# Attention and expert block on one core: the word lists of the five engines in another order

## The chip, the cores and the metric

The kernel runs on one core of one Trainium2 chip. The metric is the time of one execution on the device in microseconds (us), as the median of three runs. Engines are named as the profile names them: PE multiplies matrices, DVE is the vector engine, ACT the scalar engine, POOL is GpSimd, and SP issues DMAs.

## The reference

For 8 batches of 256 tokens with 128 channels the reference adds a gated attention and then a gated layer of experts. Attention has 16 heads of 8 channels and is the sum of a causal self-attention and a cross-attention to 256 context rows of 64 channels.

```python
x = x + tanh(g_xattn) * attention(layernorm(x), ctx)
x = x + tanh(g_ffn) * experts(layernorm(x))

def attention(x, ctx):
    y = softmax(causal(q @ k.T * scale)) @ v          # 16 heads, 256 x 256
    y = y + softmax(qc @ kc.T * scale) @ vc           # 16 heads, 256 x 256
    return y @ Wp + bp

def experts(x):
    s = sigmoid(x @ router.T)                         # 16 experts in 4 groups
    w = top 4 of s + bias within the best 2 groups    # each weight s, scaled to sum 2.5
    return sum over e of w[e] * (silu(x @ gate[e].T) * (x @ up[e].T)) @ down[e].T
```

## The kernel before

Each batch is one chain of small steps, and the steps of several batches overlap. Every step is a word `what:batch:n` (a number that is left out is 0), and the table ORDERS (lines 91 to 237) holds, for each engine, the list of the words that this engine executes, in exactly that order. Nothing else sets the order: there is no scheduler, the engines run their own lists and meet only at semaphores. PE has 717 words, DVE 391, ACT 378, SP 130 and POOL 110. If the first word in a list has to wait, all words behind it on that engine wait too.

The steps of one batch, with the lines of the work in the kernel before:

- *Prologue.* DVE takes the statistics of x (`stats1`, L1000, L1003), POOL makes the reciprocal deviation and the normalised x (`rstd1`, `xn1`, L586 to L593), PE transposes it (`xnT`, L852) and projects it (`proj`, L861 to L864; `vproj`, L879, L881). ACT copies the results out (`xnT_e`, `proj_e`, `v_e`). ACT, POOL and DVE split queries and keys into three bf16 parts (`part0`, L682; `sp1`, L412 and L415; `sp3`, L419). The second index 0 is cross, 1 is self.
- *Stacks.* SP and ACT store the parts to DRAM (`pd0`, `pd1`, `pd2`, L426, L427) and load them back as tall operands: `qst`, `kst` (L434, L437), and for the first batch's cross-attention in two halves of heads, `qh` and `kh`. The causal mask is stored as extra rows of the self stacks (`tri`, L485).
- *Row maxima.* For 28 chunks of scores (`max`, 0 to 15 cross L803, 16 to 27 self L800) PE makes 128x512 scores in one of two banks and DVE reduces them (`tmax`, L1011). Chunk k waits for the reduction of chunk k-2. PE then transposes the maxima (`shift`, L888), ACT copies them, and SP writes them into one row of the query stack (`shd`, L496, L498).
- *Exponentials.* For 28 chunks (`exp`, 0 to 15 cross L825, 16 to 27 self L822) PE makes the transposed scores, the row maximum already subtracted through the added row, and ACT exponentiates them (`exp_e`, L709). There are two banks, and chunk s waits for ACT's work on chunk s-2. Chunks 0 and 16 also wait for the landing of the row of maxima.
- *Values.* PE multiplies probabilities and values in four pieces (`pv`, L846), transposes the result back (`y`, L893), DVE divides by the sum (`m`, L1017, L1024), POOL adds the cross and self results (`yadd`, L607), PE transposes and projects (`yT`, `wp`, L901), DVE adds the residual (`x1`, L1132), which POOL prepared (`xres`, L601).
- *Experts.* Statistics (`stats2`), `rstd2` and `xn2` on POOL, transpose on PE (`xn2T`), router scores (`logits`, L908), tanh on ACT, the choice of four experts on DVE in 16 small steps (`route`, L1035 to L1083, the last one writes r_w), transpose of the weights on PE (`combT`, L912), and for pairs of experts `ga`, `up` (L918), `swish`, `tup` (L1091, L1099), the weights on POOL (`fhc`, L626) and `down` (L943); `out` (L1149) and `st` end the batch. For the weights `cout` and `cin` store them and load them back spread over partitions.

While one batch is in its exponentials, the next is in its row maxima and the one before in its experts. PE reads a bank called misc for transposes and projections: its uses are numbered in the order of PE's list, one after another.

```python
for what, b, n in order("pe"):        # each engine has such a loop
ge(pe, max_taken, b * NC1 + k - 1)    # a row-maximum chunk: two banks
ge(pe, exp_done, b * NC2 + s - 1)     # an exponential chunk: two banks
pe.wait_ge(comb_done, b + 1)          # combT: r_w of the batch is there
```

## Time and profile before

| | |
|---|---|
| runs of the kernel before | 346.58, 353.40, 349.49 us |
| median | 349.49 us |
| span of the profiled execution | 347.6 us |
| median less that span | 1.9 us |
| PE, DVE, ACT, POOL busy | 92%, 74%, 56%, 43% of the span |

The profiled execution's time is known as its span; what lies around the span in an execution is taken as the difference from the median. A row of a timeline has its start, its length, the engine and line, the operation with its output and inputs, how many were joined, and in brackets the time that the engine stood idle before it, with what ended that. L lines are those of the kernel before; in the changed one the table is two lines shorter, so every later line has a number lower by two.

### The profile page before, as it was taken

How to read it: one execution, taken by the hardware profiler on the slowest of the kernel's cores; microseconds unless marked ns; L12 is line 12 of the kernel's file. 1: busy time of each engine (PE TensorE's matmuls, PEld its weight loads, DVE VectorE, ACT ScalarE, POOL GpSimd, SP SyncE). 2: the span in 40 equal slices, each digit the busy share in tenths (PEclk: the TensorE clock that was granted, in tenths of full speed). 3: DMA queues.
4: the chain of work that ended last, by engine and by line, in shares of the span. 5: the costliest groups of instructions: out<-in, count | busy, mean ns of one | idle time of the engine just before them, and what ended most of it. 6: DMA issues, size and time to landing. Idle time of an engine off the chain costs nothing.

```text
span 347.6 us, 8679 instructions
## 1 busy us (share of the span) xinstructions
PE 318.1 (92%) x3186; PEld 247.7 (71%) x3186; DVE 256.4 (74%) x639; ACT 196.2 (56%) x399; POOL 151.1 (43%) x176
## 2 busy tenths in 40 slices
PE   1579599989999999999999999999999999978696
PEld 0455365666687788778887888787888787856665
DVE  4238666868898888988798888888889854748742
ACT  2433356767667765687637765675666467532041
POOL 3884061404470588047633494318410722903422
PEclk9856759999999999999999999999999999989999
DMA  4269674688563855537655365077156005214000
GB/s 123 68 183 188 146 194 115 145 209 187 199 151 103 184 131 149 143 96 151 147 139 133 88 172 140 20 152 183 34 124 141 0 18 90 37 50 88 16 1 15
DMA packets 32889, 40.45 MB, mean 116 GB/s; under 512 B 3440, under 2 KB 29824, under 8 KB 30368
## 3 DMA queue, kind: packets, MB, share of 16 engines
q1 hardware_dynamic: 32004, 38.46, 46.7%
q10 hardware_dynamic: 844, 1.45, 1.7%
q8 instruction: 25, 0.41, 0.5%
q14 instruction: 16, 0.13, 0.2%
HBM read 29.84 MB, written 7.45 MB: 107 GB/s over the span
## 4 chain that ended last, share of the span: by engine, by line
PE 76%; DVE 7%; DMA 6%; SPq 5%; POOL 2%; issue 2%; ACT 1%; POOLq 0%; DVEq 0%
PE bank L918 15%; PE bank L846 14%; PE bank L825 8%; PE bank L943 7%; PE bank L800 7%; PE bank L803 6%; PE bank L822 5%; DMA k_stack<-tri_k 4%; SPq L427 2%; PE bank L893 2%; DVE row_max L1011 2%; PE bank L861 2%; PE bank L852 2%; SPq L426 1%; PE bank L956 1%
## 5 line engine op out<-in xcount | busy, mean ns | idle before, releaser
L1011 DVE TENSOR_REDUCE row_max<-bank 128x2 f32<-128x512 f32 (+1 forms) x224 | 146.9, 686 | 43.0 <-PE bank L803 24.9
L709 ACT ACTIVATE probs<-bank 128x512 f32<-128x512 f32 x224 | 127.5, 595 | 57.5 <-PE bank L825 27.7
L918 PE MATMUL bank<-xn2T,w_pairs_sb 128*128 128x256 f32 x256 | 68.0, 392 | 1.5 <-issue 0.9
L846 PE MATMUL bank<-probs,v_ext 128*32 128x256 f32 (+1 forms) x1024 | 57.2, 365 | 0.0
L626 POOL TENSOR_TENSOR f_h<-f_h,comb 128x512 f32<-128x512 f32 x32 | 40.3, 1273 | 36.1 <-DMA comb<-c_scr 20.4
L803 PE MATMUL bank<-k_stack,q_stack 72*128 72x256 bf16 x256 | 49.9, 284 | 2.7 <-DVE row_max L1011 2.1
L918 PEld LDWEIGHTS bank<-xn2T,w_pairs_sb 128*128 128x128 f32 x256 | 44.7, 193 | 8.3 <-issue 2.8
L825 PE MATMUL bank<-q_stack,k_stack 73*128 73x256 bf16 x256 | 49.2, 284 | 1.0 <-DMA q_stack<-shiftT 0.9
L412 POOL TENSOR_TENSOR rest<-proj,part 128x512 f32<-128x512 f32 x14 | 16.2, 1160 | 74.7 <-ACT part L682 74.6
L846 PEld LDWEIGHTS bank<-probs,v_ext 128*32 128x32 f32 x1024 | 30.0, 112 | 19.9 <-issue 4.7
L800 PE MATMUL bank<-k_stack,q_stack 121*128 121x128 bf16 (+1 forms) x384 | 39.1, 231 | 2.4 <-DMA k_stack<-tri_k 1.9
L943 PE MATMUL bank<-w_down,f_h 128*128 128x128 f32 x256 | 35.9, 277 | 0.0
L822 PE MATMUL bank<-q_stack,k_stack 121*128 121x128 bf16 (+1 forms) x384 | 35.4, 219 | 0.1
L800 PEld LDWEIGHTS bank<-k_stack,q_stack 121*128 121x128 bf16 (+1 forms) x384 | 29.0, 103 | 8.9 <-issue 2.8
L803 PEld LDWEIGHTS bank<-k_stack,q_stack 72*128 72x128 bf16 x256 | 22.0, 100 | 16.7 <-DVE row_max L1011 8.6
L943 PEld LDWEIGHTS bank<-w_down,f_h 128*128 128x128 f32 x256 | 31.8, 191 | 0.4
L724 ACT ACTIVATE f_tanh<-bank 128x512 f32<-128x512 f32 x32 | 19.2, 599 | 22.6 <-PE bank L918 22.6
L1091 DVE SCALAR_TENSOR_TENSOR f_gate<-f_tanh,bank 128x512 f32<-128x512 f32 x32 | 21.7, 679 | 13.7 <-ACT f_tanh L724 13.7
L822 PEld LDWEIGHTS bank<-q_stack,k_stack 121*128 121x128 bf16 (+1 forms) x384 | 27.0, 98 | 5.7 <-issue 1.7
L825 PEld LDWEIGHTS bank<-q_stack,k_stack 73*128 73x128 bf16 x256 | 23.9, 102 | 6.8 <-ACT probs L709 1.4
L607 POOL TENSOR_TENSOR y<-y,y_self 128x256 f32<-128x256 f32 x8 | 5.8, 728 | 50.1 <-DVE y_self L1024 50.1
L1099 DVE TENSOR_TENSOR f_h<-f_gate,bank 128x512 f32<-128x512 f32 x32 | 21.9, 683 | 6.0 <-PE bank L918 5.1
(113 smaller groups left out, 367.9 us busy)
## 6 DMA issues: line engine op xcount, KB each, us to landing
k_stack<-k_scr SPq DMA_DIRECT2D x45, 192.0 KB
q_stack<-q_scr SPq DMA_DIRECT2D x14, 576.0 KB
comb<-c_scr SPq DMA_DIRECT2D x14, 512.0 KB, 6.7
q_scr<-part SPq DMA_DIRECT2D x46, 64.0 KB
k_scr<-part SPq DMA_DIRECT2D x46, 64.0 KB
x_in<-in_x SPq DMA_DIRECT2D x8, 128.0 KB, 2.4
w_pairs_sb<-in_w_pairs SPq DMA_DIRECT2D x1, 1024.0 KB, 7.8
out<-y_out SPq DMA_DIRECT2D x8, 128.0 KB, 1.9
```

The lines of the kernel that those rows point to most:

```text
L626: nc.gpsimd.tensor_tensor(at, at, comb[:, 2 * j:2 * j + 2, :], ALU.mult).then_inc(f_hc_done, 1)
L709: nc.scalar.activation(probs[:, seq % NP, :], exp_bank[s % 2][:, :], ACT.Exp).then_inc(exp_done, 1)
L800: last = pe.matmul(ps[:, n, kt * 128:(kt + 1) * 128], q[0:rows_used], key[0:rows_used, kt * 128:(kt + 1) * 128], start=n == 0 and kt == 0, ...
L803: last = pe.matmul(ps[:, n, :], q[0:STACK], key[0:STACK], start=n == 0, stop=n == nh - 1)
L822: last = pe.matmul(ps[:, n, qt * 128 - q0:(qt + 1) * 128 - q0], key[0:rows_used], q[0:rows_used, qt * 128:(qt + 1) * 128], start=n == 0 an ...
L825: last = pe.matmul(ps[:, n, :], key[0:STACK + 1], q[0:STACK + 1], start=n == 0, stop=n == nh - 1)
L846: last = pe.matmul(pv_bank[32 * n:32 * n + VW, col + q0:col + T], v[:, VW // 2 * odd:VW // 2 * odd + VW], weights, start=odd == 0 and kt = ...
L918: last = pe.matmul(bank_of[:, n * T:(n + 1) * T], w[:, e0:e0 + 128], xn2T[:, :], start=True, stop=True)
L943: last = pe.matmul(gate_bank[:, n * 128:(n + 1) * 128], f_h[:, j, n * 128:(n + 1) * 128], w_down[:, j, :], start=j == 0 and n == 0, stop=j ...
L1011: nc.vector.tensor_reduce(row_max[:, kind, qt, h0:h0 + nh], max_bank[k % 2][:, :].rearrange("p (h k) -> p h k", h=nh), AX.X, ALU.max).then ...
L1091: nc.vector.scalar_tensor_tensor(out=f_gate[:, :], in0=f_tanh[:, :], scalar=1.0, in1=gate_bank[:, :], op0=ALU.add, op1=ALU.mult).then_inc( ...
L1099: nc.vector.tensor_tensor(f_h[:, 2 * j:2 * j + 2, :], f_gate[:, :].rearrange("p (n x) -> p n x", n=2), up_bank[:, :].rearrange("p (n x) -> ...
```

## The change

The five lists of ORDERS hold the same words in another order. No instruction is added, removed or altered; 523 of PE's 717 words, 229 of ACT's 378, 172 of DVE's 391, 80 of POOL's 110 and 78 of SP's 130 stand at another place, most of them by a few places. Only a handful go more than ten places: `combT:0` on PE, the statistics of batches 5 and 6 on DVE, `marks:7` and `xres:5` on POOL. Core lines of the diff (PE at the start and near the end, DVE, POOL and SP):

```diff
     'pe': '''
...
-        max:0:6 xnT:2 max:0:7 max:0:8 proj:2:1 max:0:9 max:0:10 shift:0 max:0:11 proj:2 max:0:12 max:0:13 max:0:14
-        max:0:15 shift:0:2 max:0:16 max:0:17 exp:0 max:0:18 exp:0:1 max:0:19 max:0:20 exp:0:2 max:0:21 exp:0:3 exp:0:4
+        proj:1:1 max:0:8 max:0:9 max:0:10 xnT:2 max:0:11 max:0:12 max:0:13 shift:0 max:0:14 max:0:15 proj:2:1 proj:2
+        shift:0:2 max:0:16 exp:0 exp:0:1 max:0:17 max:0:18 max:0:19 exp:0:2 exp:0:3 max:0:20 max:0:21 max:0:22 exp:0:4
...
-        pv:7:1 exp:7:18 exp:7:19 up:5:2 exp:7:20 ga:5:3 exp:7:21 up:5:3 xn2T:6 exp:7:22 exp:7:23 logits:6 pv:7:2
-        combT:6 pv:7:3 ga:6 up:6 y:7:1 ga:6:1 yT:7 up:6:1 wp:7 ga:6:2 up:6:2 ga:6:3 up:6:3 xn2T:7 logits:7 down:6
+        exp:7:18 pv:7:1 up:5:2 exp:7:19 exp:7:20 ga:5:3 exp:7:21 xn2T:6 up:5:3 exp:7:22 exp:7:23 pv:7:2 logits:6
+        pv:7:3 combT:6 ga:6 up:6 y:7:1 ga:6:1 yT:7 up:6:1 wp:7 ga:6:2 up:6:2 up:6:3 ga:6:3 xn2T:7 logits:7 down:6
...
     'pool': '''
...
-        yadd:4 fhc:3 sp1:7:1 fhc:3:1 rstd2:4 xn2:4 fhc:3:2 fhc:3:3 sp3:7:1 yadd:5 xres:6 fhc:4 fhc:4:1 rstd2:5 fhc:4:2
+        fhc:3 marks:7 rstd2:4 xres:5 fhc:3:1 fhc:3:2 xres:6 xn2:4 fhc:3:3 yadd:5 fhc:4 fhc:4:1 fhc:4:2 xres:7 rstd2:5
...
     'sp': '''
-        load:0 w:0 load:1 load:2 ones:0 pd1:0 pd2:0 load:3 kh:0 pd1:0:1 pd2:0:1 kh:0:1 pd0:1 kst:0:1 tri:0 shd:0 pd2:1
-        pd1:1 pd1:1:1 pd0:1:1 pd2:1:1 shd:0:2 qst:1 kst:1 qst:1:1 shd:0:1 pd2:2 kst:1:1 tri:0:1 pd1:2 pd0:2 pd1:2:1
+        load:0 w:0 load:1 load:2 ones:0 pd1:0 pd2:0 load:3 kh:0 kh:0:1 pd2:0:1 pd1:0:1 tri:0 kst:0:1 shd:0 pd2:1 pd1:1
+        pd0:1 pd0:1:1 pd2:1:1 pd1:1:1 qst:1 shd:0:2 kst:1 qst:1:1 shd:0:1 tri:0:1 kst:1:1 pd2:2 pd0:2 pd1:2 pd1:2:1
```

Place 1, the start, POOL before, between the normalised x of batch 1 and that of batch 2 (L601 is the residual, L580 and L582 clear the values' buffer of one batch, L412 to L419 split the first self-attention's operands):

```order
L593 TENSOR_SCALAR xn<-x_in,mean,rstd 128x128 x2
L412 TENSOR_TENSOR rest<-proj,part 128x512
L415 TENSOR_SCALAR part<-rest 128x512
L419 TENSOR_TENSOR part<-rest,part 128x512
L586 TENSOR_SCALAR rstd<-mean 128x2
L588 TENSOR_TENSOR rstd<-rstd,minus_half 128x2
L593 TENSOR_SCALAR xn<-x_in,mean,rstd 128x128 x2
```

POOL now, from the residual behind the normalised x of batch 1 to the normalised x of batch 2:

```order
L599 TENSOR_TENSOR x_res<-x_in,bp_row 128x256
L578 MEMSET v_ext 128x1536
L580 MEMSET v_ext 128x32x2
L578 MEMSET v_ext 128x1536
L580 MEMSET v_ext 128x32x2
L410 TENSOR_TENSOR rest<-proj,part 128x512
L413 TENSOR_SCALAR part<-rest 128x512
L417 TENSOR_TENSOR part<-rest,part 128x512
L599 TENSOR_TENSOR x_res<-x_in,bp_row 128x256
L584 TENSOR_SCALAR rstd<-mean 128x2
L586 TENSOR_TENSOR rstd<-rstd,minus_half 128x2
L591 TENSOR_SCALAR xn<-x_in,mean,rstd 128x128 x2
```

The second clearing and the residual of batch 1 now stand in front of the normalised x of batch 2; the first clearing stood ahead of the piece shown before.

Place 1 on DVE before, from the statistics of batch 2 (row_max is the row maximum of a chunk of batch 0):

```order
L1000 BN_STATS stats<-x_in 128x6 x2
L1003 BN_AGGR mean<-stats 128x2 x2
L1011 TENSOR_REDUCE row_max<-bank 128x2
L1000 BN_STATS stats<-x_in 128x6 x2
L1003 BN_AGGR mean<-stats 128x2 x2
L1011 TENSOR_REDUCE row_max<-bank 128x2 x6
L412 TENSOR_TENSOR rest<-proj,part 128x512
L415 TENSOR_SCALAR part<-rest 128x512
L1011 TENSOR_REDUCE row_max<-bank 128x2 x4
```

DVE now, from the same statistics:

```order
L998 BN_STATS stats<-x_in 128x6 x2
L1001 BN_AGGR mean<-stats 128x2 x2
L998 BN_STATS stats<-x_in 128x6 x2
L1001 BN_AGGR mean<-stats 128x2 x2
L1009 TENSOR_REDUCE row_max<-bank 128x2 x11
L410 TENSOR_TENSOR rest<-proj,part 128x512
L413 TENSOR_SCALAR part<-rest 128x512
L417 TENSOR_TENSOR part<-rest,part 128x512
L1009 TENSOR_REDUCE row_max<-bank 128x2 x5
```

The statistics of batch 3 went from behind the first row maximum to ahead of it, and the split of batch 1's operands from behind the seventh to behind the eleventh.

Place 2, the end, PE before, around the transposed expert weights of batch 6 (L912), the last piece of values of batch 7 (L846), the experts of batch 6 (L918) and the transpose of the self result of batch 7 (L893):

```order
L943 MATMUL bank<-w_down,f_h 128x128 x4
L912 MATMUL bank<-ident,r_w 16x128 x2
L846 MATMUL bank<-probs,v_ext 32x256 x4
L846 MATMUL bank<-probs,v_ext 32x128 x4
L846 MATMUL bank<-probs,v_ext 32x256 x4
L846 MATMUL bank<-probs,v_ext 32x128 x4
L918 MATMUL bank<-xn2T,w_pairs_sb 128x256 x4
L893 MATMUL bank<-ident,y_raw 128x128 x4
```

PE now, at the same place:

```order
L941 MATMUL bank<-w_down,f_h 128x128 x6
L844 MATMUL bank<-probs,v_ext 32x256 x4
L844 MATMUL bank<-probs,v_ext 32x128 x4
L844 MATMUL bank<-probs,v_ext 32x256 x4
L844 MATMUL bank<-probs,v_ext 32x128 x4
L910 MATMUL bank<-ident,r_w 16x128 x2
L916 MATMUL bank<-xn2T,w_pairs_sb 128x256 x4
L891 MATMUL bank<-ident,y_raw 128x128 x4
```

The values went from behind the expert weights to ahead of them.

Place 2 on DVE before, the end of the routing of batch 6 (r_eout to r_w) with the division of batch 7's cross result (recip, y) in it:

```order
L1073 MATCH_REPLACE r_eout<-r_etop,r_ein 128x20 x2
L1017 RECIPROCAL recip<-bank 128x32
L1024 TENSOR_TENSOR y<-bank,recip 128x256
L1075 SCALAR_TENSOR_TENSOR r_sel<-r_eout,r_score 128x2x16
L1078 TENSOR_REDUCE r_sum<-r_sel 128x2
L1080 RECIPROCAL r_sum<-r_sum 128x2
L1083 SCALAR_TENSOR_TENSOR r_w<-r_sel,gate,r_sum 128x32
L1149 TENSOR_TENSOR y_out<-bank,x 128x256
```

DVE now, at the same place:

```order
L1071 MATCH_REPLACE r_eout<-r_etop,r_ein 128x20 x2
L1073 SCALAR_TENSOR_TENSOR r_sel<-r_eout,r_score 128x2x16
L1076 TENSOR_REDUCE r_sum<-r_sel 128x2
L1078 RECIPROCAL r_sum<-r_sum 128x2
L1081 SCALAR_TENSOR_TENSOR r_w<-r_sel,gate,r_sum 128x32
L1015 RECIPROCAL recip<-bank 128x32
L1022 TENSOR_TENSOR y<-bank,recip 128x256
L1147 TENSOR_TENSOR y_out<-bank,x 128x256
```

The division went from the middle of the routing to behind it.

Place 3, the middle, POOL before, around the second layernorm of batch 4 (rstd, xn), with the expert weights of batch 3 (f_h):

```order
L626 TENSOR_TENSOR f_h<-f_h,comb 128x512
L586 TENSOR_SCALAR rstd<-mean 128x2
L588 TENSOR_TENSOR rstd<-rstd,minus_half 128x2
L593 TENSOR_SCALAR xn<-x,mean,rstd 128x128 x2
L626 TENSOR_TENSOR f_h<-f_h,comb 128x512 x2
L419 TENSOR_TENSOR part<-rest,part 128x512
```

POOL now:

```order
L624 TENSOR_TENSOR f_h<-f_h,comb 128x512
L612 MEMSET rest 16x1024
L614 AFFINE_SELECT rest<-rest 16x1024
L584 TENSOR_SCALAR rstd<-mean 128x2
L586 TENSOR_TENSOR rstd<-rstd,minus_half 128x2
L599 TENSOR_TENSOR x_res<-x_in,bp_row 128x256
L624 TENSOR_TENSOR f_h<-f_h,comb 128x512 x2
L599 TENSOR_TENSOR x_res<-x_in,bp_row 128x256
L591 TENSOR_SCALAR xn<-x,mean,rstd 128x128 x2
L624 TENSOR_TENSOR f_h<-f_h,comb 128x512
```

Between rstd and xn of batch 4 there now stand two residuals and two steps of expert weights.

## Rows read from the trace of the kernel before

**Rows 1.** The page's first part, busy time of each engine over the span

```profile
PE 318.1 (92%) x3186; PEld 247.7 (71%) x3186; DVE 256.4 (74%) x639; ACT 196.2 (56%) x399; POOL 151.1 (43%) x176
```

**Rows 2.** Three stretches: PE, PEld, DVE, ACT, POOL busy, PE clock, DMA share, GB/s

```profile
20.00:30.00 10.00, 9.28 (x34) 6.00 (x33) 5.04 (x12) 3.82 (x9) 8.29 (x10) 0.50 0.80 194
107.00:285.00 178.00, 177.96 (x1978) 145.95 (x1979) 149.29 (x378) 116.97 (x241) 81.73 (x85) 1.00 0.50 117
285.00:347.60 62.60, 53.98 (x424) 41.98 (x412) 35.74 (x103) 22.57 (x45) 22.68 (x23) 0.97 0.21 41
```

**Rows 3.** The chain that ended last: start us, us, what

```profile
26.75 13.16 DMA k_stack<-tri_k
...
107.19 1.86 PE bank L846 x32
...
284.48 1.86 PE bank L846 x32
```

**Rows 4.** DVE timeline, first row maxima: start us, us, line, operation [idle before]

```profile
23.83 0.69 DVE L1011 TENSOR_REDUCE row_max<-bank 128x2 f32<-128x512 f32 x1 [5.93 <-PE bank L803]
...
40.77 1.29 DVE L1011 TENSOR_REDUCE row_max<-bank 128x4 f32<-128x512 f32 x2 [3.06 <-PE bank L800]
```

**Rows 5.** Waits of DVE, 42 to 75 us: total us, times, longest us

```profile
DVE row_max L1011 <- PE bank L800: 4.8, 9, 1.7
DVE row_max L1011 <- PE bank L803: 4.7, 2, 3.2
```

**Rows 6.** POOL timeline, prologues of batches 1 and 2

```profile
10.83 0.72 POOL L601 TENSOR_TENSOR x_res<-x_in,bp_row 128x256 f32<-128x256 f32 x1
...
13.87 1.38 POOL L580 MEMSET v_ext<- 128x1536 f32 x1 [1.32 <-DVE part L419]
...
22.29 1.59 POOL L593 TENSOR_SCALAR xn<-x_in,mean,rstd 128x128 f32<-128x128 f32 x2 [0.18 <-POOL rstd L588]
```

**Rows 7.** SP timeline, DMA issues of the first stacks

```profile
22.10 1.23 SPq L437 DMA_DIRECT2D k_stack<-k_scr  x3
...
33.89 0.71 SPq L496 DMA_DIRECT2D q_stack<-shiftT  x1
```

**Rows 8.** ACT timeline, issue of the first self stack

```profile
24.34 0.78 ACTq L434 DMA_DIRECT2D q_stack<-q_scr  x1
```

**Rows 9.** Exponentials by form: duration ns min/median/max, first and last start

```profile
L709 ACT ACTIVATE probs<-bank x224: 569/597/655, 41.6 to 305.1; 128x512 f32<-128x512 f32 x112
```

**Rows 10.** POOL timeline, second layernorm of batch 4

```profile
242.14 1.59 POOL L593 TENSOR_SCALAR xn<-x,mean,rstd 128x128 f32<-128x128 f32 x2 [0.18 <-POOL rstd L588]
243.70 1.28 POOL L626 TENSOR_TENSOR f_h<-f_h,comb 128x512 f32<-128x512 f32 x1
```

**Rows 11.** PE timeline, transpose of that layernorm

```profile
246.01 0.38 PE L852 MATMUL bank<-ident,xn 128*128 128x128 f32 x2
```

**Rows 12.** PE timeline near the end

```profile
298.78 0.59 PE L908 MATMUL bank<-w_model_sb,xn2T 128*128 128x16 f32 x4
299.30 1.51 PE L846 MATMUL bank<-probs,v_ext 128*32 128x256 f32 x32
...
307.96 0.38 PE L912 MATMUL bank<-ident,r_w 128*16 128x128 f32 x2 [1.91 <-DVE r_w L1083]
308.27 2.13 PE L846 MATMUL bank<-probs,v_ext 128*32 128x256 f32 x32
310.33 3.01 PE L918 MATMUL bank<-xn2T,w_pairs_sb 128*128 128x256 f32 x8
313.18 0.60 PE L893 MATMUL bank<-ident,y_raw 128*128 128x128 f32 x4
```

**Rows 13.** DVE timeline, routing near the end

```profile
306.20 0.35 DVE L1017 RECIPROCAL recip<-bank 128x32 f32<-128x32 f32 x1
306.58 0.42 DVE L1024 TENSOR_TENSOR y<-bank,recip 128x256 f32<-128x256 f32 x1
...
307.57 0.25 DVE L1083 SCALAR_TENSOR_TENSOR r_w<-r_sel,gate,r_sum 128x32 f32<-128x32 f32 x1
```

254 lines of the change are left out of this document (126 added, 128 removed).

## The prediction

> **What bounds the kernel now.** I read the page's first part, then the same engines by stretches, then the chain of waits, and only then the timelines of the engines at the places that the change touches.
>
> The first part shows PE at 318.1 of 347.6 us and DVE at 256.4 [rows 1]. A share says little about an order; the stretches say more. From 107 to 285 us PE is busy for 177.96 of 178.00 us at the full clock, while DVE has 149.29 and POOL 81.73 [rows 2]. In that stretch nothing that another engine does can come too late for PE: a word that moves there moves PE's work about and removes none. The chain gives the same as a period. The first piece of values of a batch starts at 107.19 for one batch and at 284.48 for the one five batches on [rows 3], so (284.48 - 107.19) / 5 = 35.5 us a batch, all of it PE's own work. The order can be worth something only where PE is not full: before 107 us and after 285 us. Behind 285 us PE works for 53.98 of 62.60 us, so 8.6 us are open there [rows 2].
>
> In the start three things are to be seen. The load of the first stacks keeps the DMA engines at a share of 0.80 between 20 and 30 us, at a PE clock of 0.50 [rows 2]. The self maxima of batch 0 wait for the causal mask, which was issued at 26.75 and took 13.16 us to land [rows 3]; DVE is idle for 3.06 us just there [rows 4]. And up to 75 us DVE waits for scores from PE for 4.8 + 4.7 = 9.5 us, with a longest wait of 3.2 [rows 5]: the row maxima set the pace and they are sometimes not fed.
>
> At the end the chain is one batch's routing. The router scores of batch 6 come at 298.78, the weights r_w are ready at 307.57 + 0.25 = 307.82, PE has waited 1.91 us for them at 307.96, and the last values of batch 7 and the next experts stand behind that wait [rows 12, 13].
>
> **The change, part by part.** The multiset of words is the same, so nothing is added to or taken from any engine's work; the sum is about waits alone. It is made against the profiled span, 347.6 us, and the 1.9 us between that and the median are put back at the end.
>
> *The end.* Before, the last values of batch 7 stand behind the transposed weights: 307.96 weights, 308.27 values (2.13), 310.33 experts (3.01), 313.18 transpose of the result [rows 12]. Now the values come first. PE's other words ahead of them are the same, and they end 1.91 us before 307.96, at 306.05 [rows 12]; the values fit between 306.05 and 308.2, inside the old wait. What then counts is when r_w is there. Two edits pull at it. The router scores now stand behind the third piece of values, which takes 1.51 [rows 12]; an expert word that stood ahead of the transpose before the scores goes behind it, and I charge +1.2. On DVE the division of batch 7's cross result, 0.35 + 0.42 = 0.77, goes from the middle of the routing to behind it [rows 13]: -0.77. So r_w is ready at 307.82 + 1.2 - 0.77 = 308.25. The transposed weights follow at 308.4 for 0.38, then 8 expert matrices of up to 3.01, then the transpose at 311.7 at the latest, against 313.18: a gain of 1.5. If the expert matrices run at the full clock (2.13 us of values there against 1.51 for the same 32 matrices at 299.30, both in rows 12, so a factor of 0.7), the transpose is at 310.6 and the gain is 2.6. I take 2.0. Behind the transpose the division of the self result, the residual, the second layernorm, the routing and the experts of batch 7 follow one another as before, so the gain goes through to the end. Bounds: if the experts of batch 6 are late because their weights come behind the third values too, the 1.2 costs and only the 0.77 comes back, 0.43 lost, so +0.5; if the values fill the wait wholly and the scores are not later, the 1.91 + 0.77 and some clock: -3.0.
>
> *The start.* POOL now clears both batches' value buffers and prepares a second residual ahead of the normalised x of batch 2: one clearing of 1.38 and one residual of about 0.72 more, less the 1.32 us for which POOL waits before [rows 6]. The normalised x of batch 2 thus ends about 0.8 later than 22.29 + 1.59 = 23.88, at 24.7. DVE's statistics of batch 3 wait for that x (it reads the mean that they overwrite), and they now stand ahead of the first row maximum. That one was at 23.83 [rows 4], and is now at about 25.6, a loss of 1.8; behind it are queued the 16 cross maxima, and PE's score chunks wait for these. Against this, DVE's work up to the sixteenth maximum is the same as before, and only the place of the statistics and of batch 1's split in it differs; some of the wait for the first scores is made up where DVE waited for later ones. I take the last cross maximum to end 0.6 later. SP issues the second half of the first key stack straight behind the first half, without the two pairs of part stores that stood between, which I put at 3 to 4 us before 22.10, and the mask ahead of the self keys, which I put at 2.5 us before 26.75 [rows 3, 7]. The mask's landing was at 26.75 + 13.16 = 39.9; I take 38.3. The self queries pay for it: ACT issued them at 24.34 [rows 8], and now does so behind the self projection of batch 1, for which PE first does eight score chunks, so near 32; they should land beside the mask. The row of maxima of the first half, which SP issued at 33.89 [rows 7], comes from a transpose that now stands behind three more score chunks: near 37.5, landing near 40.5 to 41, and the first exponential starts then, as before. One wait (the mask) goes and the other (that row) takes its place within about half a us. Net zero. Bounds: if the mask was all that held the stretch, the 3.06 us of DVE's wait come back, -3; if the late first maximum passes through whole and SP's six part stores, which now stand ahead of the next stack's loads, add theirs, 1.8 + about 2, +4.
>
> Here the Trainium skill bears on the sum: "DMA: Bandwidth & Descriptors", in its section on issuing engines not being separate queues, says that DMAs from SP, ACT and GpSimd end on the same 16 engines and interleave, and that issuing from several saves only issue time. The share of 0.80 [rows 2] agrees. By that rule an earlier issue of one half only delays the other, and the term of the start would be zero; by the 13.16 us of the mask alone [rows 3] it would be the 2.5 us by which the issue is earlier.
>
> *The middle.* PE has 0.04 us of idle time in 178 [rows 2], so a gain of zero is the ceiling for all words there. What could be lost is a word that becomes ready too late. On PE the exponential chunks are now mostly in pairs; one costs ACT 0.597 us [rows 9], and with two banks the second pair waits if PE has less than about 1.2 us of other work between pairs. In the list I find a values piece, two row-maximum chunks or expert words between nearly all pairs. On POOL the second layernorm of batch 4 is now split: two residuals and two weight steps stand between its two parts, 2 x 0.72 + 2 x 1.28 = 4.0 us [rows 6, 10]. Before, the normalised x ended at 242.14 + 1.59 = 243.73 and PE transposed it at 246.01 [rows 10, 11], a reserve of 2.28, so 4.0 would leave 1.7 us of waiting. But in PE's list the transpose has gone back too by some 2 us, and its router scores with it; 0.3 or less remains. I count the middle at zero; bounds 0 and +5 (three such words at 1.7).
>
> *Sum.* 347.6 - 2.0 + 0 + 0 = 345.6 us of span, and with 1.9 around it 347.5 us.
>
> **The rivals.**
> *The start is repaired.* If the paired chunks, an earlier mask and earlier prologues of the following batches keep DVE fed before 75 us, the 3.06 [rows 4] and the 9.5 [rows 5] go in part: with half, 6.3, the time is 349.5 - 6.3 - 2.0 = 341.2 us, faster. For it: PE is not full there and DVE is asked all the time. Against it: the landing of the first stacks is a matter of bytes, and the first maximum is later, not earlier.
> *Pairs of exponentials make PE stand.* The place is PE's list from 107 to 285 us, the price up to 0.597 us per pair [rows 9], and it decides where less than 1.2 us of PE work stands between two pairs. There are about 33 more adjacent pairs than before; at 0.3 each they cost 9.9 us: 349.5 - 2.0 + 9.9 = 357.4 us, slower. For it: there is no reserve in 178 us, each wait is a loss in full. Against it: the list has such work between nearly all pairs.
> *The order hardly matters.* The gain at the end is eaten by the later scores, the rest is zero: 349.5 us.
>
> **How the numbers follow.** The forecast, 347.5, gets 0.49 with a range of its own from 344 to 351; the repaired start 0.21; the pairs, with late layernorms and late loads that work the same way, 0.16; no difference 0.14. About 2%, 7.0 us, is what a measurement of this kernel can tell from no change: its three runs lie 6.8 us apart. Faster than 342.5 is the most of the repaired start and a little of the forecast, 0.22; slower than 356.5 is most of the pairs and a little of the forecast's upper end, 0.17; the rest, 0.61, lies within. The range reaches from 340 to 357: below it lies the part of the repaired start in which more than two thirds of DVE's waits go, above it the part of the pairs in which each costs over 0.3.
>
> **What would show it right or wrong.** Right at the end: PE's wait ahead of the transposed weights is under 1 us with the values ahead of it, and the transpose of batch 7's self result follows the end of batch 5's last `down` by 4.5 to 5.6 us, where it is 313.18 - 306.05 = 7.1 before. Right at the start: the mask lands before 39.9, DVE's 3.06 us shrink, but the first exponential stays near 41 and the first values at 107 stay within 2 us. Right in the middle: the period of 35.5 us stands and PE has no idle time from 107 to 285. The prediction is wrong if the first values come at 103 or earlier (the start was repaired), or if PE shows waits for probabilities, layernorms or stacks of more than 3 us between 107 and 285 (the pairs, or the late layernorms).

## The result and the profile after

| | kernel before | changed kernel |
|---|---|---|
| median of 20 runs | 350.53 us | 354.11 us |
| lowest and highest | 346.58 to 354.74 | 350.45 to 358.55 |
| span of the profiled execution | 347.6 | 349.9 |

The ratio is 1.0104 with a 95% interval of 1.0078 to 1.0131: the new order is slower by about 1.0%, 3.6 us, less than the 2% of a clear verdict but outside the noise. Ratios and intervals, here and below, leave out those executions of a kernel that took over 1.5% more than its fastest. The profiled execution of the changed kernel took 351.63 us and is one of the quicker ones, so its span shows 2.3 us of the 3.6.

The first look is again at the stretches, which answer to [rows 2]. Behind the first column are busy time and count of PE, PEld, DVE, ACT and POOL, then PE clock, DMA share and GB/s:

```profile
20.00:30.00 10.00, 5.35 (x20) 2.67 (x18) 3.67 (x9) 2.13 (x5) 5.18 (x7) 0.50 0.82 178
107.00:285.00 178.00, 177.81 (x1972) 145.89 (x1971) 148.75 (x369) 116.12 (x241) 84.57 (x88) 1.00 0.53 123
```

The stretch from 107 to 285 us is as full as before, 177.81 of 178.00 us. From 20 to 30 us PE is busy for 5.35 us where it was for 9.28. Since the middle of this execution neither gives nor takes, everything that changed can be read as a shift between the two timelines. PE's timeline, at the first and the last batch of the middle, as the chain had them in [rows 3]:

```profile
111.65 1.72 PE L844 MATMUL bank<-probs,v_ext 128*32 128x256 f32 x28
```

```profile
288.00 1.72 PE L844 MATMUL bank<-probs,v_ext 128*32 128x256 f32 x28
```

The first values of batch 2 start at 111.65 where they started at 107.12 in the same view (the chain's row is 0.07 later), so the whole loss, 4.5 us, is there before the middle begins. The period is (288.00 - 111.65) / 5 = 35.3 us, where it was 35.5. Near the end the last `down` of batch 5, which has the same 672 words ahead of it on PE in both lists, ends 4.5 us later too (310.54 against 306.05). The span ends 2.3 us later, so 2.2 of the 4.5 are given back at the end.

**The start.** PE's timeline in the first 60 us, with the idle time before a row and what ended it in brackets:

```profile
24.76 0.61 PE L801 MATMUL bank<-k_stack,q_stack 72*128 72x256 bf16 x2 [4.11 <-DMA q_stack<-q_scr]
25.16 1.06 PE L859 MATMUL bank<-xnT,w_model_sb 128*128 128x256 f32 x2
26.01 1.06 PE L861 MATMUL bank<-ctx_in,w_ctx_sb 128*128 128x256 f32 x2
...
31.47 1.06 PE L859 MATMUL bank<-xnT,w_model_sb 128*128 128x256 f32 x2
...
39.21 0.61 PE L801 MATMUL bank<-k_stack,q_stack 72*128 72x256 bf16 x2 [2.61 <-DVE row_max L1009]
...
41.00 1.06 PE L859 MATMUL bank<-xnT,w_model_sb 128*128 128x256 f32 x2
...
43.56 0.89 PE L861 MATMUL bank<-ctx_in,w_ctx_sb 128*128 128x256 f32 x2
...
44.50 0.39 PE L798 MATMUL bank<-k_stack,q_stack 121*128 121x128 bf16 x4
44.73 0.60 PE L823 MATMUL bank<-q_stack,k_stack 73*128 73x256 bf16 x4
...
54.53 1.03 PE L823 MATMUL bank<-q_stack,k_stack 73*128 73x256 bf16 x4 [2.19 <-DMA q_stack<-shiftT]
```

PE stands for 4.11 us until the first stack is there. Its queries, in the chain, took 6.49 us:

```profile
18.23 6.49 DMA q_stack<-q_scr
```

Before, the projections of batch 1 filled that time; now the one for the cross-attention is in the rows at 25.16 and 26.01, behind the chunk that waits, and the one for the self-attention at 31.47 and 32.32, between the eighth chunk and the ninth. At 39.21 PE stands for 2.61 us for a row maximum. From 41.00 to 44.45 it makes the projections of batch 2, which now stand between the last cross chunk and the first self chunk (44.50). At 54.53 it stands for 2.19 us for a row of maxima. DVE's timeline, which answers to [rows 4], and POOL's show what holds the maxima:

```profile
25.72 0.49 DVE L998 BATCH_NORM_STATS2 stats<-x_in 128x6 f32<-128x128 f32 x2 [10.50 <-POOL xn L591]
...
26.41 0.66 DVE L1009 TENSOR_REDUCE row_max<-bank 128x2 f32<-128x512 f32 x1
...
33.85 2.09 DVE L1009 TENSOR_REDUCE row_max<-bank 128x2 f32<-128x512 f32 x3 [1.44 <-PE bank L801]
35.85 0.68 DVE L410 TENSOR_TENSOR rest<-proj,part 128x512 f32<-128x512 f32 x1
...
37.03 1.52 DVE L417 TENSOR_TENSOR part<-rest,part 128x512 bf16<-128x512 f32 x1
...
40.70 1.29 DVE L1009 TENSOR_REDUCE row_max<-bank 128x2 f32<-128x512 f32 x2 [0.16 <-PE bank L801]
44.93 1.36 DVE L1009 TENSOR_REDUCE row_max<-bank 128x4 f32<-128x512 f32 x2 [2.94 <-PE bank L798]
```

```profile
11.76 2.58 POOL L591 TENSOR_SCALAR xn<-x_in,mean,rstd 128x128 f32<-128x128 f32 x2 [0.18 <-POOL rstd L586]
...
24.02 1.59 POOL L591 TENSOR_SCALAR xn<-x_in,mean,rstd 128x128 f32<-128x128 f32 x2 [0.18 <-POOL rstd L586]
36.65 1.35 POOL L410 TENSOR_TENSOR rest<-proj,part 128x512 f32<-128x512 f32 x1 [11.04 <-ACT part L680]
38.09 1.81 POOL L413 TENSOR_SCALAR part<-rest 128x512 bf16<-128x512 f32 x1
```

The first row maximum starts at 26.41 instead of 23.83. PE's first chunk was done at 24.76 + 0.61 = 25.37, but DVE was still in front of the statistics of batch 3, which waited until 25.7 for POOL's normalised x of batch 2 (24.02 + 1.59 = 25.61). The cross maxima end at 40.70 + 1.29 = 41.99 instead of 34.63 + 3.08 = 37.71, by the row of the kernel before:

```profile
34.63 3.08 DVE L1011 TENSOR_REDUCE row_max<-bank 128x2 f32<-128x512 f32 x5
```

Between the eighth maximum and the ninth, at 33.85, DVE stands for 1.44 us until PE is through with the projection at 31.47 and the ninth chunk. The two halves of batch 1's split now stand together between two maxima, from 35.85 to 37.03 + 1.52 = 38.55. PE's wait of 2.61 us lies in that time, but DVE works through it without a gap. At 44.93 DVE stands for 2.94 us, nearly the 3.06 that it stood for the mask before.

SP's timeline, which answers to [rows 7]:

```profile
25.01 0.65 SPq L483 DMA_DIRECT2D k_stack<-tri_k  x1
...
40.67 0.72 SPq L494 DMA_DIRECT2D q_stack<-shiftT  x1
...
49.13 0.68 SPq L494 DMA_DIRECT2D q_stack<-shiftT  x1
```

And the last row of the view of the mask's tile:

```profile
DMA to landing us min/median/max: 8.5/8.5/8.5
```

The mask was issued at 25.01 and landed 8.5 us later, at 33.5, 11 us ahead of its first use at 44.50. The first row of maxima left at 40.67 (33.89 before), and the second at 49.13 (40.58 before), behind six part stores and the next query stack.

**The end.** PE's timeline, which answers to [rows 12]:

```profile
304.77 0.62 PE L906 MATMUL bank<-w_model_sb,xn2T 128*128 128x16 f32 x4
...
308.98 1.56 PE L941 MATMUL bank<-w_down,f_h 128*128 128x128 f32 x12
310.47 1.51 PE L844 MATMUL bank<-probs,v_ext 128*32 128x256 f32 x32
312.87 0.39 PE L910 MATMUL bank<-ident,r_w 128*16 128x128 f32 x2 [0.90 <-DVE y L1022]
313.25 1.97 PE L916 MATMUL bank<-xn2T,w_pairs_sb 128*128 128x256 f32 x8
315.05 0.60 PE L891 MATMUL bank<-ident,y_raw 128*128 128x128 f32 x4
```

and DVE's, the last steps of the routing and of the division behind it, which answers to [rows 13]:

```profile
311.84 0.25 DVE L1081 SCALAR_TENSOR_TENSOR r_w<-r_sel,gate,r_sum 128x32 f32<-128x32 f32 x1
...
312.39 0.42 DVE L1022 TENSOR_TENSOR y<-bank,recip 128x256 f32<-128x256 f32 x1
```

The last values now run at 310.47, PE waits 0.90 us (before 1.91) ahead of the transposed weights at 312.87, and the transpose of batch 7's self result comes at 315.05. It is 1.87 us later than before, not 4.5. What ends the wait of 0.90 us is not r_w, which is ready at 311.84 + 0.25 = 312.09, but the division of batch 7's cross result (y, L1022). It reads the bank misc, and the transposed weights are that bank's next use, so PE can't start them before it.

### The profile page after: what moved, and what is told of

Same layout as the page of the kernel before. It is cut to its first block, busy times and chain, and to the rows that moved or that the text cites. A ratio compares the mean times of both kernels' runs of the same rounds, so it can differ in the third digit from the quotient of the medians.

```text
span 349.9 us, 8679 instructions
## 1 busy us (share of the span) xinstructions
PE 317.0 (91%) x3186; PEld 246.4 (70%) x3186; DVE 253.0 (72%) x639; ACT 194.6 (56%) x399; POOL 152.5 (44%) x176
## 4 chain that ended last, share of the span: by engine, by line
PE 71%; DMA 9%; DVE 7%; SPq 5%; issue 4%; POOL 3%; ACT 1%; ACTq 0%; POOLq 0%; DVEq 0%
PE bank L916 14%; PE bank L844 13%; PE bank L801 9%; PE bank L941 7%; PE bank L823 6%; PE bank L820 6%; PE bank L798 4%; DMA q_stack<-q_scr 4%; DVE row_max L1009 2%; DMA k_stack<-k_scr 2%; SPq L425 2%; PE bank L859 2%; PE bank L891 2%; DMA q_stack<-shiftT 2%; SPq L424 1%
## 5 line engine op out<-in xcount | busy, mean ns | idle before, releaser
L707 ACT ACTIVATE probs<-bank 128x512 f32<-128x512 f32 x224 | 125.5, 595 | 59.8 <-PE bank L823 31.8
L916 PE MATMUL bank<-xn2T,w_pairs_sb 128*128 128x256 f32 x256 | 66.6, 387 | 3.0 <-issue 1.6
L801 PE MATMUL bank<-k_stack,q_stack 72*128 72x256 bf16 x256 | 49.0, 291 | 8.5 <-DMA q_stack<-q_scr 4.1
L844 PE MATMUL bank<-probs,v_ext 128*32 128x256 f32 (+1 forms) x1024 | 56.0, 360 | 0.0
L916 PEld LDWEIGHTS bank<-xn2T,w_pairs_sb 128*128 128x128 f32 x256 | 44.0, 190 | 9.8 <-issue 3.8
L823 PE MATMUL bank<-q_stack,k_stack 73*128 73x256 bf16 x256 | 43.7, 277 | 2.3 <-DMA q_stack<-shiftT 2.2
L798 PE MATMUL bank<-k_stack,q_stack 121*128 121x128 bf16 (+1 forms) x384 | 35.1, 221 | 1.4 <-DVE row_max L1009 1.0
L820 PE MATMUL bank<-q_stack,k_stack 121*128 121x128 bf16 (+1 forms) x384 | 34.2, 220 | 0.3 <-ACT probs L707 0.3
L798 PEld LDWEIGHTS bank<-k_stack,q_stack 121*128 121x128 bf16 (+1 forms) x384 | 26.8, 99 | 6.3 <-DVE row_max L1009 3.1
```

Source lines behind the costliest of these rows:

```text
L707: nc.scalar.activation(probs[:, seq % NP, :], exp_bank[s % 2][:, :], ACT.Exp).then_inc(exp_done, 1)
L798: last = pe.matmul(ps[:, n, kt * 128:(kt + 1) * 128], q[0:rows_used], key[0:rows_used, kt * 128:(kt + 1) * 128], start=n == 0 and kt == 0, ...
L801: last = pe.matmul(ps[:, n, :], q[0:STACK], key[0:STACK], start=n == 0, stop=n == nh - 1)
L820: last = pe.matmul(ps[:, n, qt * 128 - q0:(qt + 1) * 128 - q0], key[0:rows_used], q[0:rows_used, qt * 128:(qt + 1) * 128], start=n == 0 an ...
L823: last = pe.matmul(ps[:, n, :], key[0:STACK + 1], q[0:STACK + 1], start=n == 0, stop=n == nh - 1)
L844: last = pe.matmul(pv_bank[32 * n:32 * n + VW, col + q0:col + T], v[:, VW // 2 * odd:VW // 2 * odd + VW], weights, start=odd == 0 and kt = ...
```

## The experiments

From the rows above came two theories for the start and one rival for the whole. Rival: the middle or the end loses, through pairs of exponentials. Theory A: work of batch 1 (the projections on PE, later its split on DVE) stands in the middle of the row maxima of batch 0. Theory B: the second half of the first stack, brought forward, delays the first half. Later theory C: the first row maximum is held by the statistics ahead of it, which wait for POOL. All runs but e1 and e2 carry the new order with a few words moved. The diffs show words of ORDERS against the changed kernel.

The table collects what the texts below use. The times are from the profiled executions' timelines, the ratios against the kernel before from the runs.

| run | first row maximum | end of cross maxima | first values of batch 2 (shift) | ratio | 95% interval |
|---|---|---|---|---|---|
| kernel before | 23.83 | 37.71 | 107.12 | | |
| changed kernel | 26.41 | 41.99 | 111.65 (+4.5) | 1.0104 | 1.0078 to 1.0131 |
| e1, old start, new rest | 23.23 | 35.19 | 107.14 (0.0) | 0.9943 | 0.9906 to 0.9979 |
| e2, new start, old rest | 26.01 | 41.03 | 113.93 (+6.8) | 1.0193 | 1.0126 to 1.0261 |
| e3, projections ahead | 26.08 | 39.64 | 110.57 (+3.5) | 1.0055 | 1.0019 to 1.0092 |
| e4, second half later | 26.01 | 41.03 | 111.51 (+4.4) | 1.0063 | 1.0024 to 1.0101 |
| e5, statistics and POOL | 24.77 | 41.36 | 112.10 (+5.0) | 1.0102 | 1.0021 to 1.0184 |
| e6, e4 and e5 | 21.95 | 41.12 | 112.16 (+5.0) | 1.0113 | 1.0031 to 1.0194 |
| e7, e3, e4 and e5 | 23.18 | 37.30 | 108.79 (+1.7) | 0.9993 | 0.9954 to 1.0033 |
| e8, e7 and the split | 22.92 | 35.94 | 106.75 (-0.4) | 0.9940 | 0.9897 to 0.9983 |
| e9, e3 and the split | 26.11 | 38.64 | 110.02 (+2.9) | 0.9994 | 0.9959 to 1.0030 |
| e10, e4, e5 and the split | 22.39 | 36.97 | 108.00 (+0.9) | 0.9990 | 0.9948 to 1.0032 |
| e11, e8 and an earlier row | 23.08 | 36.10 | 109.81 (+2.7) | 1.0054 | 1.0013 to 1.0095 |
| e12, values behind again | 26.12 | 40.32 | 114.64 (+7.5) | 1.0194 | 1.0133 to 1.0255 |

The changed kernel and e12 have the same lists up to the end, yet their cross maxima end 1.7 us and their values of batch 2 start 3.0 us apart. The kernel before and e1 share the old start, and their cross maxima end 2.5 us apart. So far can two executions of one order differ, and smaller differences of two single traces are not taken as effects below, unless rows account for them. PE's clock has a part in it. From 60 to 70 us, in the changed kernel and then in e12:

```profile
60.00:70.00 10.00, 9.53 (x106) 5.72 (x104) 8.39 (x15) 7.61 (x15) 0.84 (x1) 1.00 0.87 177
```

```profile
60.00:70.00 10.00, 9.34 (x76) 4.64 (x74) 5.13 (x8) 4.18 (x9) 0.00 (x0) 0.66 0.82 159
```

PE was busy for about as long, but at a granted clock of 0.66 it got through 76 matrix products where it did 106 at 1.00. The first values of batch 0 had come at 54.16 in e12 and at 55.92 in the changed kernel, so e12 was still ahead there.

**e1: where the loss and the gain lie.** Every word that started in the first 62 us of the kernel before keeps its old order; the rest is new.

```diff
     'pe': '''
-        xnT:0 proj:0 proj:0:1 vproj:0 xnT:1 vproj:1 max:0 proj:1 max:0:1 max:0:2 max:0:3 max:0:4 max:0:5 max:0:6 max:0:7
+        xnT:0 proj:0 vproj:0 proj:0:1 xnT:1 proj:1 proj:1:1 max:0 max:0:1 max:0:2 vproj:1 max:0:3 max:0:4 max:0:5
...
```

> All words that ran in the first 62 us of the kernel before stand in the old order, everything behind them in the new one. If the new order loses about 4.5 us in the start and gives back about 2.2 at the end (theory), this is 2.2 us faster than the kernel before, a ratio of 0.994, with its first row maximum near 23.8 us and the first values of batch 2 near 107. If the loss comes from the pairs of exponentials in the middle (rival), it is slower than before, above 1.005, and PE has waits between 107 and 285 us.

Measured: 0.9943, the forecast 0.994, with the values of batch 2 at 107.14. Together with the ratio of the changed kernel this puts the loss in the start: the same rest with the new start is at 1.0104.

**e2: the reverse.** New order for the words of the first 62 us, old order behind.

```diff
     'pe': '''
...
-        pv:7:3 combT:6 ga:6 up:6 y:7:1 ga:6:1 yT:7 up:6:1 wp:7 ga:6:2 up:6:2 up:6:3 ga:6:3 xn2T:7 logits:7 down:6
+        combT:6 pv:7:3 ga:6 up:6 y:7:1 ga:6:1 yT:7 up:6:1 wp:7 ga:6:2 up:6:2 ga:6:3 up:6:3 xn2T:7 logits:7 down:6
...
```

> The reverse: the words of the first 62 us in the new order, everything behind them in the old one. Theory: 4.5 us slower than the kernel before, a ratio of 1.013, with the whole loss there at 75 us and the transpose of batch 7's self result near 313.2 + 4.5 = 317.7. Rival (loss in the middle or at the end): a ratio of 1.000 to 1.004.

Measured: 1.0193, more than expected though 1.013 is just within the interval; PE is busy from 107 to 285 us for 177.96 of 178.00 here, and the transpose of batch 7's self result comes at 320.40, not near 317.7. The rival is out as the cause: with the old middle the loss is there, and with the new middle and the old start (e1) it is not. In the trace the old continuation has 6.8 us of delay at batch 2, the new one 4.5, but two single executions do not settle that the new continuation makes up for some of the late start.

**e3 and e4: the projections alone, the second half alone.**

The first two pairs of lines are e3 (PE, ACT), the last two e4 (SP, ACT).

```diff
-xnT:1 vproj:1 max:0 proj:1 max:0:1 max:0:2 max:0:3 max:0:4 max:0:5 max:0:6 max:0:7 proj:1:1
+xnT:1 proj:1 proj:1:1 vproj:1 max:0 max:0:1 max:0:2 max:0:3 max:0:4 max:0:5 max:0:6 max:0:7
-qh:0 qh:0:1 v_e:1 proj_e:1 part0:1 proj_e:1:1 qst:0:1
+qh:0 qh:0:1 proj_e:1 part0:1 proj_e:1:1 qst:0:1 v_e:1
...
-kh:0 kh:0:1 pd2:0:1 pd1:0:1
+kh:0 pd2:0:1 pd1:0:1 kh:0:1
-qh:0 qh:0:1 v_e:1
+qh:0 v_e:1 qh:0:1
```

> The new order, but both projections of batch 1 stand on PE ahead of the first score chunk again, and their copies on ACT ahead of the values' copy. If the loss of the start is that PE stands idle for 4.1 us at the first stack with the projections queued behind it (theory A), PE's wait there falls to about 1 us, the last cross maximum ends 1.7 to 2.5 us sooner than 42.0, and the time is about 2 us below the new order, 1.004 to 1.006 of the kernel before. If the landing of the first half alone decides (theory B), the first chunk stays at 24.8 and the time within 0.5 us of the new order, 1.010.

> The new order, but the second half of the first cross stack is issued later again: the keys behind a pair of part stores on SP, the queries behind the values' copy of batch 1 on ACT. Theory B (the second half, brought forward, delays the landing of the first): the first chunk comes at 23.2 to 23.8 instead of 24.8, and the time is 1.0 to 1.6 us below the new order, 1.006 to 1.007 of the kernel before. Theory A (the projections): the first chunk may move, but the last cross maximum stays within 0.5 us of 42.0 and the time at 1.010.

Measured: e3 1.0055, e4 1.0063; both are as their own theory wants, and both intervals reach into that of the changed kernel. The traces say more. In e3 PE's wait for the first stack falls from 4.11 to 1.88 us, DVE no longer stands for the ninth chunk, and the cross maxima end 2.4 us sooner than in the changed kernel, 1.4 sooner than in e2, which has the changed kernel's start. In e4 the first chunk does come sooner, by 2.9 us against the changed kernel and by 1.9 against e2 (23.73), as PE's row shows, and nothing comes of it, as DVE's rows show:

```profile
21.82 0.61 PE L801 MATMUL bank<-k_stack,q_stack 72*128 72x256 bf16 x2 [1.56 <-DMA q_stack<-q_scr]
```

```profile
25.32 0.49 DVE L998 BATCH_NORM_STATS2 stats<-x_in 128x6 f32<-128x128 f32 x2 [10.50 <-POOL xn L591]
...
26.01 5.44 DVE L1009 TENSOR_REDUCE row_max<-bank 128x2 f32<-128x512 f32 x8
```

The chunk is ready at 21.82 + 0.61, but the maximum starts at 26.01, because DVE's list has the statistics first and these wait for POOL until 25.3. First maximum and end of the cross maxima are those of e2. So theory B is true of the chunk, and in the traces its price is nil as long as the next lock holds; that e4's ratio is 0.4% under the changed kernel's is not clear of the intervals.

**e5 and e6: the statistics, alone and with the second half.**

e5 is the edit below, first on DVE and then on POOL; e6 is e4 and e5.

```diff
-stats1:2 stats1:3 tmax:0 tmax:0:1
+stats1:2 tmax:0 stats1:3 tmax:0:1
-rstd1:1 xn1:1 xres:0 vclear:0 vclear:0:1 sp1:0:1 sp3:0:1 xres:1 rstd1:2 xn1:2
+xres:0 rstd1:1 vclear:0 xn1:1 sp1:0:1 sp3:0:1 rstd1:2 xn1:2 vclear:0:1 xres:1
```

> The new order, but on DVE the statistics of batch 3 stand behind the first row maximum again, and POOL's list up to the normalised x of batch 2 is the old one. Theory C (the first row maximum is held by these statistics, which wait for POOL): it starts right behind its chunk, near 25.4 instead of 26.4, and the time falls by about 1 us, to 1.007 of the kernel before. Rival (the landing of the stack sets it, theory B): by 0.3 us or less.

> Both edits: the second half issued later and the statistics and POOL's list as before. With the second half alone the first chunk came at 21.8 and the first maximum at 26.0, held by the statistics. If two locks in a row hold the first maximum (theory B and C together), it now starts near 22.5 to 23, 3.5 us sooner than in the new order, and the last cross maximum ends at 38.5 to 39.5 instead of 42.0; the time falls by 2 to 3 us, to 1.002 to 1.005. If the projections on PE set the pace behind (theory A alone), the last cross maximum stays above 41 and the time at 1.008 to 1.010.

Measured: 1.0102 and 1.0113. In e5 the first maximum starts at 24.77, the chunk's landing being the lock again, but the time doesn't fall to theory C's 1.007, and the cross maxima end at 41.36: a miss. In e6 the first maximum starts at 21.95, 4.5 us sooner than in the changed kernel, and the cross maxima still end at 41.12. That was a miss for B with C, but one with a flaw of the run's own, in PE's timeline:

```profile
32.36 1.01 PE L801 MATMUL bank<-k_stack,q_stack 72*128 72x256 bf16 x4 [2.42 <-issue]
```

In e6 the second half's queries were issued behind the values' copy of batch 1, at 25.07, and PE stood 2.42 us for that half at 32.36 (the trace names only "issue"; the row is the ninth chunk, the first of the second half). PE's wait of 2.61 us for a row maximum, at 38.34 here, stood as well.

**e7 and e8: all three, and the split.**

e7 is e3, e4 and e5, with the second half's queries behind `part0:1`; e8 is e7 and, on DVE:

```diff
-tmax:0:6 tmax:0:7 tmax:0:8 tmax:0:9 tmax:0:10 sp1:1 sp3:1
+tmax:0:6 sp1:1 tmax:0:7 tmax:0:8 tmax:0:9 tmax:0:10 sp3:1
```

> The projections ahead, the second half later, the statistics and POOL's list as before, all else in the new order. If these three are the whole loss: last cross maximum near 37.7, first exponential near 41, 0.994 to 0.996 of the kernel before. If SP's six part stores ahead of the second row of maxima cost by themselves (PE waits 2.2 us for it at 54.5 in the new order), the first chunk of batch 1 stays 1.5 to 2.5 us behind 53.5, and the time is 0.999 to 1.003.

> As the last, and on DVE the first half of batch 1's split stands behind the seventh row maximum again, not behind the eleventh with the second half at its back. If the two steps together hold PE's chunks (2.6 us in the new order, at 39.2), the wait falls under 1.5 us and the last cross maximum ends 0.5 to 1.2 us sooner than in the run with the three edits alone; otherwise by less than 0.3.

Measured: e7 0.9993, e8 0.9940, and the cross maxima end at 37.30 and 35.94. The place of the split, in PE's timeline of e7 and then of e8, and DVE's of e8:

```profile
34.51 0.61 PE L802 MATMUL bank<-k_stack,q_stack 72*128 72x256 bf16 x2 [2.61 <-DVE row_max L1010]
```

```profile
33.16 0.61 PE L802 MATMUL bank<-k_stack,q_stack 72*128 72x256 bf16 x2 [0.59 <-DVE row_max L1010]
```

```profile
31.81 0.68 DVE L418 TENSOR_TENSOR part<-rest,part 128x512 bf16<-128x512 f32 x1
```

The wait falls from 2.61 to 0.59 us, and the cross maxima end 1.36 us sooner, 0.26 of which are there at the first maximum already. The third step of the split, alone between two maxima, takes 0.68 us, where it took 1.52 beside POOL's split of the self operands; that is 0.84 of the rest. The two ran 12 times each in one session, with medians of 349.47 and 347.84 us. e7's time is the one expected for the six part stores, and its first chunk of batch 1 starts at 56.22, 2.7 us behind 53.5; but e8 has the same stores in the same places, and its first chunk is at 54.06. The interval of e8 is clear of that of the changed kernel; with these four moves undone the new order is as fast as with the whole old start.

**e9 and e10: leaving out one repair or the other.**

e9 is e3 and e8's edit on DVE. e10 is e5, e8's edit on DVE, and of e4 the edit on SP alone:

```diff
-kh:0 kh:0:1 pd2:0:1 pd1:0:1
+kh:0 pd2:0:1 pd1:0:1 kh:0:1
```

> The new order with two repairs: the projections of batch 1 ahead of the score chunks on PE, and the first half of its split behind the seventh row maximum on DVE. If work of batch 1 in the middle of the row maxima is the larger part of the loss (theory A with the split), the last cross maximum ends at 38.3 to 39 instead of 42.0, the values of batch 2 start 2 to 3 us sooner than 111.65, and the time is 1.001 to 1.004 of the kernel before; what is left is the late first maximum, 26.0 instead of 23.8. If the first maximum is the larger part (theory B with C), the last cross maximum ends above 39.6 and the time is at 1.006 or more.

> The new order with the other repairs: second half later (this time its queries ahead of the values' copy on ACT, since in the run with the values' copy ahead they were issued at 25.07 and PE stood 2.4 us for them), statistics and POOL's list as before, the split on DVE as before, but the projections of batch 1 still behind the first and the eighth chunk. Theory A: the first maximum is at 22 but the projections hold the chunks, the last cross maximum ends at 38.5 to 40, and the time is 1.002 to 1.006. Theory B with C: it ends under 37.7 and the time is 0.994 to 0.998.

Measured: 0.9994 and 0.9990. Both intervals lie below that of the changed kernel (from 1.0078 on) and reach into that of e8. e9's cross maxima end where theory A with the split expects them, and its time is at that theory's lower edge or below; the values of batch 2 came 1.6 us sooner, not 2 to 3. e10 fell between the two branches: its cross maxima end at 36.97, as B with C wants, its time is worse than that. e9's profiled execution took 358.06 us, 7.5 more than the median of its runs; from 107 to 285 us PE is busy for 177.99 of 178.00 there and from 315 on its clock is 0.79, so the delay lies behind the rows used here. No single repair of the start (e3, e4, e5) is clear of the changed kernel's interval; e7, e9 and e10, which undo two or three of the four groups, are, by about 1.1%.

**e11: one lock further.**

e11 is e8 and, on SP:

```diff
-shd:0 pd2:1 pd1:1 pd0:1 pd0:1:1 pd2:1:1 pd1:1:1 qst:1 shd:0:2 kst:1
+shd:0 pd2:1 pd1:1 pd0:1 shd:0:2 pd0:1:1 pd2:1:1 pd1:1:1 qst:1 kst:1
```

> The run with all repairs (0.994 of the kernel before), and on SP the second row of maxima behind three of the six part stores instead of behind all of them and the next query stack. PE waited 3.2 us for this row at 49.5. If that wait is on the path, the first chunk of batch 1 and the values of batch 2 come 1 to 3 us sooner than 54.1 and 106.75, and the time is 0.985 to 0.991. If the stack of batch 1, which is now issued 0.7 us later, decides there, the wait only moves and the time stays at 0.993 to 0.997.

Measured: 1.0054. PE's waits from 17 to 110 us (line, releaser, total us, times, longest us):

```profile
PE bank L802 <- DMA k_stack<-k_scr: 3.8, 1, 3.8
```

The 3.2 us for the row are gone, and 3.8 us for the key stack of batch 1 are there instead. The first chunk of batch 1 starts at 53.94, where it was at 54.06 in e8. The wait moved, as the second branch has it; that the time became worse than e8's by 1% was expected by neither. The traces show where the 3 us arise that are there at the values of batch 2 (109.81 against 106.75). The stretch behind the wait, in e8 and then in e11:

```profile
54.00:62.00 8.00, 7.55 (x83) 4.13 (x80) 5.81 (x10) 5.45 (x11) 1.68 (x2) 1.00 0.96 181
```

```profile
54.00:62.00 8.00, 8.00 (x54) 4.73 (x58) 4.65 (x7) 3.37 (x6) 0.00 (x0) 0.50 0.87 191
```

PE, which has stood for 3.8 us until 53.94, runs in e11 at a granted clock of 0.50 and gets through 54 matrix products in these 8 us, where e8 has 83 at 1.00. So a wait that only moves can cost more in its new place. This is one execution of each; that the other runs of e11 lose their 1% in the same way is not shown.

**e12: the end.**

On PE alone:

```diff
-pv:7:3 combT:6 ga:6
+combT:6 pv:7:3 ga:6
```

> The new order, with the last values of batch 7 behind the transposed weights of batch 6 again and nothing else. If the gain at the end comes from values that fill the wait for the weights, the transpose of batch 7's self result comes 1.4 to 2.1 us later than 315.05, PE's wait ahead of the weights grows from under 1 to over 2 us, and the time is 1.014 to 1.016 of the kernel before. If the gain comes from the earlier weights or the clock, the transpose moves by less than 0.5 us.

Measured: 1.0194. The profiled execution was later than the changed kernel's by 3.0 us at batch 2 and by more in the middle, for no word that differs, so only distances within its end are used. PE's timeline, and the middle of that execution as a stretch:

```profile
315.42 1.56 PE L941 MATMUL bank<-w_down,f_h 128*128 128x128 f32 x12
319.14 0.39 PE L910 MATMUL bank<-ident,r_w 128*16 128x128 f32 x2 [2.17 <-DVE y L1022]
319.45 1.51 PE L844 MATMUL bank<-probs,v_ext 128*32 128x256 f32 x32
320.89 1.99 PE L916 MATMUL bank<-xn2T,w_pairs_sb 128*128 128x256 f32 x8
322.72 0.60 PE L891 MATMUL bank<-ident,y_raw 128*128 128x128 f32 x4
```

```profile
107.00:285.00 178.00, 174.76 (x1938) 142.40 (x1937) 147.89 (x371) 114.55 (x236) 80.25 (x83) 1.00 0.54 125
```

The wait ahead of the weights is 2.17 us (0.90 in the changed kernel), and from the weights to the transpose of batch 7's self result it takes 322.72 - 319.14 = 3.58 us, against 315.05 - 312.87 = 2.18. The values in the wait are worth 1.4 us from the weights on. From the end of the last `down` of batch 5 (315.42 + 1.56 = 316.98, and 308.98 + 1.56 = 310.54) the transpose is 5.74 us away here, 4.51 in the changed kernel: 1.2. In the trace the theory holds, at or just under the lower bound of its 1.4 to 2.1 us. The time lies above its 1.014 to 1.016, which the interval (from 1.0133) takes in; the 0.9%, 3.2 us, by which it is over the changed kernel's is more than twice what the rows of the end show, and the rest is not explained.

## Why the prediction was wrong

**The forecast of 347.5 us, a small gain, went the wrong way.** The time is a loss of 1.0%. The terms of the middle and the end were right, the start's, put at zero, was 4.5 us, half a us past its own upper bound of +4.

*The middle: right in the profiled execution, with less reserve than said.* The sum had zero there. PE is busy for 177.81 of 178.00 us, the period is 35.3 us, and PE shows no wait for probabilities there, by which the rival of the pairs, 357.4 us, would have been known. But in e12's execution, with the same words in the same order, PE is busy for 174.76 of the 178: it waited for stacks, a row of maxima and POOL's steps, 0.4 to 1.0 us each. The profiles of the ten other runs with the new middle have 177.08 to 178.00, those with the old middle (before, e2) 177.96. So the zero holds but for single executions, which can lose some 3 us, and the median's 3.6 us against the profile's 2.3 may hold some of that; this was not tried.

*The end: right in size, and only half for the reason given.* The sum had -2.0. From the last `down` to the transpose of the self result it was 7.13 us before and is 4.51 now, 2.6 less; e1 measures -0.57%, which is -2.0 us, with an interval from -0.7 to -3.3. By e12 the order's own part is 1.2 of that 2.6 in the trace. The other 1.4 is the clock. The stretch from the weights to the transpose, in the kernel before and in e12:

```profile
308.30:313.20 4.90, 4.90 (x42) 3.40 (x42) 0.13 (x1) 1.57 (x3) 0.00 (x0) 0.65 0.36 102
```

```profile
319.10:323.00 3.90, 3.86 (x45) 2.85 (x46) 0.62 (x2) 1.57 (x3) 0.00 (x0) 1.00 0.03 7
```

The granted clock was 0.65 before, so partly at the lower of its two levels (1.2 GHz), and 1.00 in e12. The values took 2.13 us before and 1.51 in e12, the 8 expert matrices 3.01 and 1.99, together 1.64 less, of which e12 loses 0.26 again by a longer wait. The prediction had that difference only as a possible bonus. It goes with the order of the end, since the same rows took 2.24 and 2.90 us in e2, the other execution with the old end, and 1.51 and 1.96 to 1.99 in all twelve with the new one; but e12 shows that it does not hang on the place of these values, and which word it hangs on was not tried. Of the two edits that pull at r_w, the scores came 6.0 us later than before, of which 4.5 are the start's: 1.5, where 1.2 was charged. r_w follows them by 311.84 + 0.25 - 304.77 = 7.32 us against 9.04, 1.7 less, where the division's 0.77 was charged; one step of the routing that took 1.30 us before took 0.17. The 0.77 itself did not reach PE. The sum had the transposed weights follow r_w at once, as before (307.82 and 307.96), but they come 0.78 us behind it now, when the division that was moved out of its way has left the bank misc.

*The start: the failed step is "I take the last cross maximum to end 0.6 later".* It ended 4.3 later. By the rows 2.58 us of that are the later first maximum, and the other 1.70 are that the sixteen maxima took longer: 15.58 us from the first to the end of the last, 13.88 before. Three terms under it were wrong or left out.

First, the late first maximum was put at +1.8 and came at +2.6. The lock was the one named, the statistics that wait for POOL's x of batch 2. But this x ended at 25.61, not at 24.7: POOL's normalisation of batch 1 had taken 2.58 us (11.76), while DVE split batch 0's operands, and that of batch 2 took 1.59 (24.02). The first chunk came 1.6 us late as well, with the second half of the stack going out beside the first, but that is covered by the lock: in e4 the chunk comes sooner and the first maximum does not.

Second, the text let the delay be made up "where DVE waited for later ones". DVE waits more now. The 1.44 us ahead of its ninth maximum, behind the self projection of batch 1, are in the changed kernel and in e2, e4, e5 and e12, which have that word at the same place, and gone in e3, e7, e8 and e9, which have it ahead of the chunks. The split in one piece has a smaller part: undoing it shortens the sixteen maxima from 13.56 to 12.53 us (e9 against e3) and from 14.12 to 13.02 (e8 against e7), and 0.84 of that is the step that now meets POOL's work. In e12 it does not meet it, takes 0.69, and the sixteen take 14.20.

Third, the projections of batch 1 were counted only for the self queries that they delay. That they left PE nothing to do during 4.11 us of waiting and then stood in front of later chunks was not counted at all, though the order of the list says so. That these moves make the loss is shown by e8, which undoes them; the division of the 4.3 us is read from single executions.

*The mask.* "One wait goes and the other takes its place within half a us" had the right shape and the wrong second wait. The mask came even sooner than taken, 33.5 instead of 38.3, and PE no longer waits for it. The row of maxima that was to take its place went out at 40.67, not near 37.5, but PE shows no wait for it. What stands there are the projections of batch 2, for which the sum has no term: they were spread among the cross chunks before, and now PE is busy with them from 41.00 to 44.45, behind the last cross chunk. The first self chunk and the first exponential, at 44.73 and not near 41, follow without a wait, and DVE stands for 2.94 us. No run moves these words. In e8 they still stand there, and DVE stands for 3.50 us at 39.44; what they cost is open. In the old start it was the mask that set this place: e1 ends its cross maxima 2.5 us sooner than the kernel before, and its first self chunk starts at 40.34, where that of the kernel before starts at 40.15. The gain of a wait removed is bounded by what comes next, and what came next had itself become later.

*The rule on the DMAs.* The prediction weighed the Trainium skill, "DMA: Bandwidth & Descriptors", section "Issuing engines are not separate DMA queues", which says that DMAs of all issuing engines share the same engines and interleave. The trace agrees: the first queries took 6.49 us to land with the second half beside them, and e4, with the second half later, had the first chunk 1.9 to 2.9 us sooner than e2 and the changed kernel. The weighing drew the wrong thing from it, a zero term: the half which is needed first paid for the other. In the changed kernel that price is hidden by the statistics; with these out of the way (e5 against e6) it is 24.77 against 21.95 at the first maximum.

*What stays open.* How the loss divides among the four groups. Three of them undone alone move little (e3 to e5), and the split was not undone alone. e7, e9 and e10, which leave one or two of the groups as in the new order, lie half a per cent above e8, within intervals of 0.4% to a side; the four overlap, so that no sum of parts is given here. In e9 and e10 the statistics on DVE, POOL's list and the second half were not parted. Why the executions of one order spread by several us in the start was not tried; the granted clock has a part in it, as the rows of the changed kernel and e12 show, but what makes it differ between them is open.

## What to carry to other kernels

When all engines run fixed lists, read a reordering as locks in a row: for each step that waits, which word stands at the head of each list it needs, and what it waits for. Undoing one lock shows little while the next one holds (e4, e5), so put back all the suspects at once first, and then leave out one at a time. In the start and the end, where PE is not full, a word that could fill a wait and goes behind the word that waits leaves the wait empty: at the end the filled wait was worth 1.2 to 1.4 us. In the middle, where PE is full, the same shuffling cost 0.2 us of 178 in the changed kernel's profile. And when a step is moved out of another's way, see whether it now holds something that the other's reader needs, as the division holds the bank misc. The best order here is the new one with the old start (e1, 0.9943) or with the four moves undone (e8, 0.9940): clear of the changed kernel, and 0.6% faster than the kernel before, which is less than the 2% of a clear verdict.

## What the runs showed of the hardware

A step on DVE that reads two tiles took 0.68 us alone (e8, 31.81) and 1.52 us beside POOL's work on two tiles of the same kind (the changed kernel, 37.03); POOL's steps stretched as well, from 1.15 and 1.50 (e8) to 1.35 and 1.81. The Trainium skill, "GPSIMD Engine Reference", section "1. Specifications", states that GpSimd shares its interfaces to SBUF with VectorE and that they contend where a DVE instruction has two SBUF inputs; the rows agree.

Three issues of the self keys on SP, which took 1.46 us together in the kernel before, took 5.05 right behind the two mask stores, in SP's timeline of the changed kernel:

```profile
26.16 5.05 SPq L435 DMA_DIRECT2D k_stack<-k_scr  x3
```

SP's list stood for that time. It cost nothing here, because SP's next word waited for its row of maxima anyway. What in the stores held the issues up is not shown.

Behind a wait of 3.8 us PE ran at a granted clock of 0.50, the lower of its two levels (1.2 GHz), from 54 to 62 us (e11), and 32 matrix products of values took 3.62 us (59.73), where they took 1.93 in e8 (58.36) at 1.00.
